# Blocks moved in 2 KB pieces and in four parts between the stack's parts, and one bias load per graph

## What is computed

```python
def layer(h, bias, Wq, Wk, Wv, bv, Wo, bo):            # h (32, 256, 384), bias (32, 256, 256)
    q, k = (h @ Wq.T).reshape(b, n, 12, 32), (h @ Wk.T).reshape(b, n, 12, 32)
    v = (h @ Wv.T + bv).reshape(b, n, 12, 32)
    s = einsum('bqhd,bkhd->bhqk', q, k) * 384 ** -0.5 + bias[:, None]
    s = where(any(s != 0, axis=-1, keepdims=True), s, -inf)
    p = nan_to_num(softmax(s, axis=-1))
    return einsum('bhqk,bkhd->bqhd', p, v).reshape(b, n, 384) @ Wo.T + bo

x = x + layer(relu(layernorm(x)), adj + adj, *weights_0)
x = x + layer(relu(layernorm(x)), adj, *weights_1)
```

## Time and profile before

| | us |
|---|---|
| median of 3 runs | 1669.72 (1667.43 to 1672.46) |
| the profiled execution | 1675.96 |
| its span | 1674.2 |
| PE busy | 1579.8 (94%) |
| ACT busy | 1360.3 (81%) |
| DVE busy | 1352.4 (81%) |
| GpSimd (POOL) busy | 1316.7 (79%) |
| granted TensorE clock | 0.99 of full speed |
| share of the 16 DMA engines on the core's queue | 67.8% |

### The profile page before, as it was taken

The page is one execution under the profiler, slowest core; times in us unless marked ns, Lnnn a source line. Parts: engine busy times, 40 slices in busy tenths (PEclk is TensorE's granted clock), DMA queues, the critical chain, the costliest instruction groups (busy, mean ns, idle before and its releaser), DMA issues.

```text
span 1674.2 us, 45828 instructions
## 1 busy us (share of the span) xinstructions
PE 1579.8 (94%) x13184; PEld 1406.6 (84%) x13184; DVE 1352.4 (81%) x4934; ACT 1360.3 (81%) x4297; POOL 1316.7 (79%) x1673
## 2 busy tenths in 40 slices
PE   5999999999999999999999999999999999999997
PEld 5888888888888888888888888888888888888885
DVE  6787888888788888787888888878788878878884
ACT  5887887888788888878888888878788888887885
POOL 4778788788778788787877787877887878877885
PEclk9999999999999999999999999999999999999998
DMA  8667667667667677676676776766766766767754
GB/s 242 145 149 176 156 155 176 147 165 175 145 164 165 147 175 162 152 171 145 164 172 152 168 165 150 171 157 152 176 155 156 175 148 162 172 140 172 161 126 112
DMA packets 174010, 268.62 MB, mean 160 GB/s; under 512 B 30912, under 2 KB 132800, under 8 KB 173760
## 3 DMA queue, kind: packets, MB, share of 16 engines
q1 hardware_dynamic: 173760, 265.68, 67.8%
HBM read 34.87 MB, written 12.58 MB: 28 GB/s over the span
## 4 chain that ended last, share of the span: by engine, by line
PE 38%; SPq 37%; DMA 16%; issue 5%; ACT 2%; DVE 1%; POOL 0%; ACTq 0%; POOLq 0%; DVEq 0%
SPq L234 26%; DMA stack<-split_qk 16%; PE misc_bank L720 12%; SPq L242 11%; PE score_bank L646 6%; PE misc_bank L764 4%; PE probT_bank L658 4%; PE misc_bank L739 4%; PE values_bank L666 4%; PE values_bank L675 3%; ACT prob L390 1%; ACT probT L402 1%; PE misc_bank L700 1%; PE values_bank L752 1%; DMA prob<-w0k 0%
## 5 line engine op out<-in xcount | busy, mean ns | idle before, releaser
L390 ACT ACTIVATE prob<-neg,guard 128x256 f32<-128x256 f32 x1536 | 763.0, 509 | 0.1
L541 DVE CUSTOM_DVE_ANT_0 neg<-score_bank,bias 128x256 f32<-128x256 f32 x1536 | 572.9, 414 | 44.3 <-PE score_bank L646 44.0
L309 POOL TENSOR_TENSOR half<-neg 128x256 f32<-128x256 f32 x768 | 547.9, 738 | 33.9 <-DVE guard L541 24.3
L402 ACT ACTIVATE probT<-probT_bank 128x512 f32<-128x512 f32 x512 | 298.1, 596 | 90.1 <-PE probT_bank L658 89.4
L646 PE MATMUL score_bank<-stack 96*128 96x256 f32 x1536 | 335.2, 308 | 37.6 <-DMA stack<-split_qk 32.5
L658 PE MATMUL probT_bank<-identity,prob 128*128 128x128 f32 x2048 | 311.6, 275 | 32.9 <-ACT prob L390 22.9
L390 ACT ACTIVATION_READ_ACCUMULATOR prob<-neg,guard 128x1 f32 x1536 | 308.2, 201 | 0.0
L658 PEld LDWEIGHTS probT_bank<-identity,prob 128*128 128x128 f32 x2048 | 240.5, 140 | 57.0 <-ACT prob L390 29.5
L646 PEld LDWEIGHTS score_bank<-stack 96*128 96x128 f32 x1536 | 230.8, 191 | 64.0 <-DMA stack<-split_qk 51.0
L314 POOL TENSOR_TENSOR half<-half 128x512 f32<-128x512 f32 x192 | 247.4, 1289 | 15.1
L438 ACT ACTIVATE split_qk<-misc_bank 128x512 fp32r<-128x512 f32 x192 | 114.0, 594 | 111.3 <-DMA stack<-split_qk 96.5
(11 more groups left out here) (92 smaller groups left out, 3994.9 us busy)
## 6 DMA issues: line engine op xcount, KB each, us to landing
stack<-split_qk SPq DMA_DIRECT2D x768, 192.0 KB, 4.1
moved<-blocks SPq DMA_DIRECT2D x1024, 64.0 KB, 2.0
bias<-adj SPq DMA_DIRECT2D x64, 256.0 KB, 4.2
rows<-x SPq DMA_DIRECT2D x32, 384.0 KB, 4.4
out<-rows SPq DMA_DIRECT2D x32, 384.0 KB, 4.8
neg<-w0q SPq DMA_DIRECT2D x1, 576.0 KB, 4.5
prob<-w0k SPq DMA_DIRECT2D x1, 576.0 KB, 6.9
probT<-w0v SPq DMA_DIRECT2D x1, 576.0 KB, 8.0
```

What stands on the lines that cost most here:

```text
L309: nc.gpsimd.tensor_tensor(half[:, step % GROUP, :, :], n[:, :, 0:N // 2], n[:, :, N // 2:N], ALU.add).then_inc(half_done, 1)
L390: nc.scalar.activation(prob[:, step % PROB, q, :], neg[:, step % NEG, q, :], ACT.Exp, scale=-1.0, bias=guard[step // GROUP][:, step % GROU ...
L402: nc.scalar.activation(probT[:, n % PROBT, :, :].rearrange("p a b -> p (a b)"), probT_bank[n % 2][:, :], ACT.Copy).then_inc(act_copy_done, 1)
L541: nc.vector.tensor_tensor_reduce(out=neg[:, step % NEG, q, :], in0=score_bank[step % 2][:, q * N:(q + 1) * N], in1=bias[u.k % 3][:, q, :], ...
```

## The change

`blocks` and `moved` are laid out with the quadrant ahead of the key tile, so the share of one quadrant for another is one piece of 2 KB in each partition, where it was two of 1 KB. There are still 16 DMAs of 64 KB, but `move_blocks` issues four (one value of `to`) at a time, and SP's list for a slot puts the four parts between the parts of the stack. For this each turn of DVE is made by two instructions of half the size. `normed` gets memory of its own, and ACT no longer waits for moves ahead of it. `bias` has four buffers and is loaded once for each graph. The store of the result comes behind the last quadrant of the stack instead of ahead of it. The lists of the other engines are the same.

```diff
-        bias = [sb(f"bias{i}", [P, TILES, N]) for i in range(3)]
+        bias = [sb(f"bias{i}", [P, TILES, N]) for i in range(GRAPHS)]
...
-        blocks = sb("blocks", [P, TILES, QUADS, MOVED * TILES * HEAD])
-        moved = sb("moved", [P, TILES, QUADS, MOVED * TILES * HEAD])
-        normed = blocks[:, :, :, :].rearrange("p a b c -> p (a b c)")[:, 0:TILES * H].rearrange(
-            "p (i c) -> p i c", i=TILES)
+        blocks = sb("blocks", [P, QUADS, TILES, MOVED * TILES * HEAD])
+        moved = sb("moved", [P, QUADS, TILES, MOVED * TILES * HEAD])
+        normed = sb("normed", [P, TILES, H])
...
-            def load_bias(u):
-                sync.wait_ge(neg_done, u.before(3).count(2 * HEADS, 2 * HEADS))
-                sync.dma_start(bias[u.k % 3][:, :, :],
+            def load_bias(u, _=0):
+                if u.t >= GRAPHS:
+                    sync.wait_ge(neg_done, Unit(max(2 * (u.t - GRAPHS) + 2, 3), UNITS).count(2 * HEADS, 2 * HEADS))
+                sync.dma_start(bias[u.t % GRAPHS][:, :, :],
...
-            def move_blocks(u):
+            def move_blocks(u, to):
                 if u.k == 0:
                     sync.wait_ge(vo_low_done, 2)
                 sync.wait_ge(heads_ready, u.before(1).count(PARTS, 2))
                 sync.wait_ge(blocks_done, u.count(MOVED, MOVED))
-                for to in range(QUADS):
-                    for of in range(QUADS):
-                        sync.dma_start(moved[to * HEAD:(to + 1) * HEAD, :, of, :],
-                                       blocks[of * HEAD:(of + 1) * HEAD, :, to, :]).then_inc(blocks_moved[to], 16)
+                for of in range(QUADS):
+                    sync.dma_start(moved[to * HEAD:(to + 1) * HEAD, of, :, :],
+                                   blocks[of * HEAD:(of + 1) * HEAD, to, :, :]).then_inc(blocks_moved[to], 16)

             def stack_quadrant(u, g):
+                sync.wait_ge(qk_low_done, u.count(CH, CH))
...
             def slot(attend, project, output, norm):
-                if norm is not None and norm.k > 1:
-                    load_bias(norm)
-                    if norm.layer == 0:
-                        load_rows(norm)
-                if attend is not None:
-                    move_blocks(attend)
-                if project is not None:
-                    sync.wait_ge(qk_low_done, project.count(CH, CH))
-                    for g in range(QUADS - 1):
-                        stack_quadrant(project, g)
-                if output is not None and output.layer == 1:
-                    sync.wait_ge(result_done, output.count(TILES, TILES))
-                    sync.dma_start(out[output.t].rearrange("(i p) c -> p i c", p=P),
-                                   rows_of(output)[:, :, :]).then_inc(stored[output.t % GRAPHS], 16)
-                if project is not None:
-                    stack_quadrant(project, QUADS - 1)
+                for stage, u, i in (
+                    (load_bias, norm, 0), (load_rows, norm, 0), (move_blocks, attend, 0), (move_blocks, attend, 1),
+                    (stack_quadrant, project, 0), (move_blocks, attend, 2), (stack_quadrant, project, 1),
+                    (move_blocks, attend, 3), (stack_quadrant, project, 2), (stack_quadrant, project, 3),
+                    (store, output, 0),
+                ):
...
                 act.wait_ge(rowsT_ready, u.count(TILES, 0))
-                for moves in blocks_moved:
-                    act.wait_ge(moves, u.before(2).count(16 * QUADS, 16 * QUADS))
...
             def turn_blocks(u, step):
-                dve.wait_ge(exp_done, u.count(2 * HEADS, 2 * step + 2))
                 for moves in blocks_moved:
                     dve.wait_ge(moves, u.before(1).count(16 * QUADS, 16 * QUADS))
-                dve.wait_ge(rowsT_ready, min(u.count(TILES, 2 * TILES), UNITS * TILES))
                 n = TILES * HEAD
-                to = blocks[:, :, :, step * n:(step + 1) * n].rearrange("p k a (q i) -> p q (k a) i", q=TILES)
-                nc.vector.transpose(to, prob[:, step % PROB, :, :].rearrange("p q (b i) -> p q b i", i=HEAD)
-                                    ).then_inc(blocks_done, 1)
+                for q in range(TILES):
+                    dve.wait_ge(exp_done, u.count(2 * HEADS, 2 * step + q + 1))
+                    at = step * n + q * HEAD
+                    of = prob[:, step % PROB, q, :].rearrange("p (k a i) -> p a k i", k=TILES, a=QUADS)
+                    turn = nc.vector.transpose(blocks[:, :, :, at:at + HEAD], of)
+                turn.then_inc(blocks_done, 1)
```

More of the change, by code:

```diff
@@ L140, in build @@
         rows_loaded = [sem(f"rows_loaded{i}") for i in range(GRAPHS)]
-        bias_loaded = [sem(f"bias_loaded{i}") for i in range(3)]
+        bias_loaded = [sem(f"bias_loaded{i}") for i in range(GRAPHS)]
         blocks_moved = [sem(f"blocks_moved{i}") for i in range(QUADS)]
@@ L210, in load_weights, with load_rows @@
                                weights[l, n].rearrange("(c p) o -> p c o", p=P)).then_inc(w_loaded[i % 4], 16)
-            def load_bias(u):
-                sync.wait_ge(neg_done, u.before(3).count(2 * HEADS, 2 * HEADS))
-                sync.dma_start(bias[u.k % 3][:, :, :],
+            def load_bias(u, _=0):
+                if u.t >= GRAPHS:
+                    sync.wait_ge(neg_done, Unit(max(2 * (u.t - GRAPHS) + 2, 3), UNITS).count(2 * HEADS, 2 * HEADS))
+                sync.dma_start(bias[u.t % GRAPHS][:, :, :],
                                adj[u.t].rearrange("(i p) k -> p i k", p=P)
-                               ).then_inc(bias_loaded[u.k % 3], 16)
-            def load_rows(u):
+                               ).then_inc(bias_loaded[u.t % GRAPHS], 16)
+            def load_rows(u, _=0):
                 sync.wait_ge(stored[u.t % GRAPHS], 16 * (u.t // GRAPHS))
@@ L243, in stack_quadrant, with store @@
                                    quad[:, q:k + 1:k - q, :]).then_inc(stacked[g], 16)
+            def store(u, _):
+                sync.wait_ge(result_done, u.count(TILES, TILES))
+                sync.dma_start(out[u.t].rearrange("(i p) c -> p i c", p=P),
+                               rows_of(u)[:, :, :]).then_inc(stored[u.t % GRAPHS], 16)
             first, second = Unit(0, UNITS), Unit(1, UNITS)
@@ L263, in slot @@
             def slot(attend, project, output, norm):
-                if norm is not None and norm.k > 1:
-                    load_bias(norm)
-                    if norm.layer == 0:
-                        load_rows(norm)
-                if attend is not None:
-                    move_blocks(attend)
-                if project is not None:
-                    sync.wait_ge(qk_low_done, project.count(CH, CH))
-                    for g in range(QUADS - 1):
-                        stack_quadrant(project, g)
-                if output is not None and output.layer == 1:
-                    sync.wait_ge(result_done, output.count(TILES, TILES))
-                    sync.dma_start(out[output.t].rearrange("(i p) c -> p i c", p=P),
-                                   rows_of(output)[:, :, :]).then_inc(stored[output.t % GRAPHS], 16)
-                if project is not None:
-                    stack_quadrant(project, QUADS - 1)
+                for stage, u, i in (
[4 more added lines that the diff above has]
+                ):
+                    if u is None or stage in (load_bias, load_rows) and (u.layer == 1 or u.k < 2):
+                        continue
+                    if stage == store and u.layer == 0:
+                        continue
+                    stage(u, i)
             program(slot)
@@ L534, in negate_scores @@
                 if step == 0:
-                    dve.wait_ge(bias_loaded[u.k % 3], bias_count(u))
+                    dve.wait_ge(bias_loaded[u.t % GRAPHS], 16 * (u.t // GRAPHS + 1))
                 dve.wait_ge(scores_done, u.count(HEADS, step + 1))
@@ L542, in negate_scores @@
                         out=neg[:, step % NEG, q, :], in0=score_bank[step % 2][:, q * N:(q + 1) * N],
-                        in1=bias[u.k % 3][:, q, :], scale=-2.0 if u.layer == 0 else -1.0, scalar=LARGEST,
+                        in1=bias[u.t % GRAPHS][:, q, :], scale=-2.0 if u.layer == 0 else -1.0, scalar=LARGEST,
                         op0=ALU.add, op1=ALU.min, accum_out=guard[step // GROUP][:, step % GROUP, q, 0:1]
@@ L672, in weigh_moved @@
                 for k in range(TILES):
-                    blocks_of = moved[:, k, :, :].rearrange("p a (h q i) -> p h q a i", h=MOVED, q=TILES)
+                    blocks_of = moved[:, :, k, :].rearrange("p a (h q i) -> p h q a i", h=MOVED, q=TILES)
                     for h in range(MOVED):
@@ L811 @@
     from concourse.bass_utils import run_bass_kernel_spmd
-    nc = bacc.Bacc("TRN2", target_bir_lowering=False, num_devices=1, dynamic_dma_scratch_size=1024)
+    nc = bacc.Bacc("TRN2", target_bir_lowering=False, num_devices=1, dynamic_dma_scratch_size=512)
```

2 lines of the change are left out of this document (removed).

## The result

The changed kernel takes 1812.5 us (median of 4 runs, 1807.93 to 1815.03); the kernel before took 1671.09 us beside it (4 runs, 1667.43 to 1673.21). The ratio is 1.085, with a 95% interval of 1.081 to 1.088. The prediction was 1755 us with a range of 1690 to 1830: the direction and the loop that causes it were right, the size was 57 us short.

A forecast was written before the change was run, and what follows sets the result against it. Bound now: the loop through moves, stack and PE, 25.50 us a slot. The stack's loop becomes 26.1 + 0.7 + 0.1 = 26.9; 1.4 us in 62 slots, +86 on 1669.7, gives 1755 us, range 1690 to 1830.

The forecast's parts named there:

- Which loop becomes the bound: Per slot: loop A (moves, stack, PE), 25.37 us, gives way to loop B (stack, `qk_high`, `qk_low`), 22.9 to 23.6 before.
- 9.2 us from `qk_high` to the last `qk_low`: ACT and DVE part of the stack's loop, read as 9.21 and 9.09 us in two slots, taken as 9.2.
- The moves cost issues and not data: SP's moves inside the stack's loop: 0.64 us per issue counted, the 0.29 us of data each hidden by it.
- Issues behind copies in flight: Moves issued behind three stack copies: 0.35 us extra per group, 0.7 together, bounds nothing to 1.7; loop 26.1 to 26.8 us.
- The handovers between stages: Quadrant 0, moves part 2, quadrant 1, part 3: 2 x 4.44 us from issue times, no separate term for changing stage.
- The last six copies: Quadrants 2 and 3 of the stack in a row: 3.72 us to the last issue, 4.17 to its landing, 7.89.
- long issues: The 14 issues ahead of the last six could pay up to 0.9 us a slot; 0.1 taken, giving 26.9.
- Pieces, `bias` and half turns at nothing: 2 KB pieces at most 0.3 us a slot, half turns 0.63 covered by 1.4 us, `bias` load ahead of waiting moves: nothing.
- The memory of `normed` at nothing: Own memory for `normed` takes away waits that did not stall ACT, so nothing was counted.
- DVE's wait for the moves: DVE's first turn of the next unit waits some 0.3 us for the last moves, hidden by 1.4; above 1.7 adds.
- Slower still: Rival: every issue behind copies pays in full, long ones too: 28.2 us a slot, +167, 1837 us; 15 in 100.
- Faster: Rival: data, not issues, pace loop B; stack's start to ACT's 16.0 us, loop 25.2, total 1651 us; 12 in 100.

## Why the prediction was right, step by step

- **Which loop becomes the bound: right.** Two loops were read from the trace of before, one of 25.4 us and one with some 2 us to spare. The change took work from the first and put it into the second. The waits, the chain, and above all the run with two buffers for `split_qk` show it. My reading "SP stands idle for some 5 us" is 5.2 in the slot shown, and "about 300 us in all" is 338.
- **9.2 us from `qk_high` to the last `qk_low`: right,** 9.28 on the mean.
- **The moves cost issues and not data: right,** by the run with half the bytes.
- **Issues behind copies in flight, 0.7 us: nearly right, 0.76.** The four moves behind three copies took 0.37 and 0.39 us more to issue than four at the median of 0.591, where I had 0.35 a group. Nearly all of it is in the second move (0.94 and 1.00 us at the median), not in the first, which I had put nearest to the fourth copy of the earlier trace rows.
- **The handovers between stages: a term that I had at nothing.** From the start of one quadrant to the next it took 4.96 and 5.00 us (means of 62 slots), where I had 4.44 + 0.35 = 4.79. Most of the rest stands between the last issue of one stage and the first of the next: 0.10 us (1016.43 behind 1014.19 + 2.13, 1019.04 behind 1016.43 + 2.51), where my sum had the 0.04 of two issues in a row.
- **The last six copies, 7.89 us: too small,** by 0.39. From the start of quadrant 2 to ACT's start they took 8.38 us on the mean, against 7.89 and some 0.1: 3.81 to the last issue, 4.47 to its landing, 0.10 to ACT. I took them from the head of one burst of before. Over all slots of the kernel before, the sixth copy is issued 3.72 us after the first and lands 4.36 us later, so my slot, with 4.17, was a quick one: that is half of the 0.39. The slot shown above is a slow one, with 5.04. What the other 0.2 us are stays open; half the bytes in the moves left them as they were.
- **In sum** the stretch from the stack's start to ACT was 18.34 us, where I had 17.7; the loop 27.65 where I had 26.9. That is 46 us of the miss in 62 slots, spread over the terms above, of which none is off by more than 0.4 us; the 0.1 for long issues is part of these means. The other 11 us are between a profiled execution and the median: before, it was 6.2 us above its median, and the one of the changed kernel was 4.6 below.
- **Pieces, `bias` and half turns at nothing: right within a per cent.** The pieces and half turns together gave 0.5% in the old order. In the new one all of these together make no clear difference (a ratio of 1.085 against 1.087 with 1 KB pieces, whole turns and three buffers of `bias`, the intervals overlap).
- **The memory of `normed` at nothing: right for the whole change, wrong as a reason.** I looked at whether the old wait stalled ACT in the old order. It would have in the new one, for 226 us.
- **DVE's wait for the moves: too small, but hidden as I said.** I had 0.3 us; it is 83.9 / 57 = 1.5 us in the slots in which it shows. It stays behind the stack's loop, and becomes the bound at once when that loop is cut, at 25.5 us.
- **The rivals.** "Slower still", at 1837 us, came nearer to the measured time than the forecast, but not by its reason: it had 1.7 us for issues behind copies, and they cost 0.76. "Faster" needed less than 16.2 us from the stack's start to ACT's; it was 18.3.

## What to carry to other kernels

Where engines hand work to each other in a fixed order, find every loop that closes from one round to the next, add up its parts, and note its spare: an issue that is moved off the longest loop lands on another, and only the longer of the two counts. Of the placements run here the best is the one in which both loops are nearly even (14 ahead and 2 inside): 3% faster than the kernel before, 2% faster than the changed kernel with all 16 ahead (0.971 against 0.989) and 10% faster than eight and eight. When a change removes a wait that never stalled, ask whether it would stall in the new order before costing it at nothing.

## What was new about the hardware

A small SBUF-to-SBUF DMA costs its queue the same with 64 KB and with 32 KB: 591 ns at the median. The second one behind three copies of 192 KB costs 0.94 to 1.00 us, with either size. In both groups of the changed kernel its issue ends 0.13 us before the copy three places ahead of it lands (medians of 62 slots, from the trace's landings), and with half the bytes 0.13 to 0.14. In the kernel before, the issues of the fourth to the eighth copy of a burst end 0.12 to 0.16 us before the copy three places ahead lands. This looks like an issue that is held until an earlier DMA is almost through. It does not hold for every issue: the third move's, for one, ends some 0.5 us before that.

The granted TensorE clock is 0.985 over the changed kernel but 0.892 with three parts inside, where PE stands nearly idle for some 5 us of each slot: in the slot shown it falls to 0.50 at the end of the stall and stays there for the first 4 us of full work behind it, so the stall costs time once more. With the order alone, where PE waits 349 us in all for ACT's normalise, it is 0.902. In the changed kernel, whose stalls are shorter, it fell to 0.50 in eight of the 62 slots, for 27 us in all; in a slot read closely it was 1.00 (1029 to 1034, PE busy for 3.37 of 5 us).
